# Attention and expert kernel: one row maximum moved a slot up, q's high parts spread over slots, fourth maximum earlier, preamble reordered

## The reference, cut to what matters

```python
x = x + xattn(ctx, layernorm(x), ...)      # x: 2 x 1024 x 256, ctx: 2 x 77 x 256
x = x + ffn(layernorm(x), ...)

# xattn, 16 heads of 64
q = lat @ Wq                               # lat: normalized x
k, v = split(concat([ctx_n, lat], axis=1) @ Wkv)     # 1024 + 77 keys
attn = softmax(q @ k.T / 8)
out = (attn @ v) @ Wout
# ffn: a shared SwiGLU expert, and 32 experts with top-4 routing within 4 of 8 groups, capacity 160
```

## Time and profile before

| | |
|---|---|
| Runs | 1634.35 us median (1633.24 to 1637.85) |
| Profiled execution | 1635.06 us; span 1633.3 us; granted TensorE clock 0.981 on average |
| PE busy | 1511.4 us (93%) |
| PE weight loads | 1060.9 us (65%) |
| DVE busy | 1051.9 us (64%) |
| ACT busy | 798.7 us (49%) |
| POOL busy | 940.4 us (58%) |
| First score product (L939) | at 51.9 us |
| Attention, first to last block | 51.9 to about 1105 us |
| Length of a block | plain 28.4 to 31.4 us, project 36.2 to 37.8 us |
| Work that ended last | PE 66%, DVE 19%, ACT 8% of the span |

### The profile page before, as it was taken

How to read it: one execution, slowest core, us unless ns; L and a number is a source line. 1 busy time by engine, 2 the same in 40 slices (tenths; PEclk the granted TensorE clock), 3 DMA queues, 4 the chain that set the end, 5 groups by cost and what they waited for, 6 DMA issues and landing times.

```text
span 1633.3 us, 23810 instructions
## 1 busy us (share of the span) xinstructions
PE 1511.4 (93%) x8086; PEld 1060.9 (65%) x8086; DVE 1051.9 (64%) x1574; ACT 798.7 (49%) x1501; POOL 940.4 (58%) x751
## 2 busy tenths in 40 slices
PE   3899999999999999999999999988889999999995
PEld 2565555555655555555555555546779999999995
DVE  6556666576666665767767776556756666666662
ACT  3345444544454445544454444534336666666662
POOL 4457666676566665665668768784433433344333
PEclk8899999999999999999999999999999999999998
DMA  3033440000000000000011000111246666667664
GB/s 95 22 81 72 101 91 11 24 15 10 24 15 10 15 10 24 15 11 15 10 28 32 27 28 27 36 39 59 85 159 175 188 185 169 174 186 188 169 174 89
DMA packets 99282, 117.93 MB, mean 72 GB/s; under 512 B 10595, under 2 KB 78181, under 8 KB 99173
## 3 DMA queue, kind: packets, MB, share of 16 engines
q1 hardware_dynamic: 82149, 96.97, 20.4%
q0 software_dynamic: 17056, 19.97, 6.3%
HBM read 74.93 MB, written 35.06 MB: 67 GB/s over the span
## 4 chain that ended last, share of the span: by engine, by line
PE 66%; DVE 19%; ACT 8%; POOL 3%; issue 3%; DMA 1%; SPq 0%; DVEq 0%; ACTq 0%; POOLq 0%
PE ps_o L954 11%; PE ps_t L811 8%; PE ps_m L811 8%; PE ps_st L811 7%; DVE arena_r L1314 7%; PE ps_m L916 7%; PE ps_st L939 5%; PE ps_st L943 4%; ACT arena_r L1574 3%; PE ps_m L848 3%; PE ps_o L848 3%; DVE arena L1325 2%; PE ps_t L974 2%; PE ps_t L1021 2%; PE ps_t L961 2%
## 5 line engine op out<-in xcount | busy, mean ns | idle before, releaser
L751 POOL TENSOR_TENSOR arena<-arena 128x512 f32<-128x512 f32 (+1 forms) x512 | 660.2, 1291 | 337.7 <-ACT arena L1597 300.2
L1597 ACT ACTIVATE arena<-ps_st 128x512 f32<-128x512 f32 (+1 forms) x576 | 329.9, 596 | 460.8 <-PE ps_st L943 426.4
L1314 DVE TENSOR_REDUCE arena_r<-ps_m 128x1 fp32r<-128x1107 f32 x256 | 334.2, 1306 | 182.8 <-PE ps_m L916 180.7
L786 POOL DMA_INDIRECT acc_rows<-arena,ids x96 | 150.8, 1571 | 268.1 <-ACT arena L1660 240.4
L954 PE MATMUL ps_o<-arena 128*64 128x512 f32 (+1 forms) x1152 | 276.5, 606 | 0.0
L939 PE MATMUL ps_st<-arena_r 128*128 128x512 f32 (+1 forms) x576 | 247.2, 429 | 13.9 <-ACT arena L1597 13.9
L943 PE MATMUL ps_st<-arena_r 68*128 68x512 f32 (+2 forms) x576 | 231.1, 401 | 2.5 <-DVE arena_r L1321 1.4
L916 PE MATMUL ps_m<-arena_r 128*128 128x370 f32 x768 | 192.6, 359 | 34.6 <-DVE arena_r L1314 27.1
L916 PEld LDWEIGHTS ps_m<-arena_r 128*128 128x128 f32 x768 | 130.9, 192 | 109.5 <-DVE arena_r L1314 68.5
L939 PEld LDWEIGHTS ps_st<-arena_r 128*128 128x128 f32 (+1 forms) x576 | 106.8, 185 | 108.1 <-ACT arena L1597 83.5
L811 PE MATMUL ps_m<-arena_r 128*128 128x320 f32 (+1 forms) x864 | 164.7, 326 | 2.1 <-DVE arena_r L1404 1.2
(11 more groups left out here) (211 smaller groups left out, 1922.7 us busy)
## 6 DMA issues: line engine op xcount, KB each, us to landing
arena<-in_L_ffn_wg_dram SPq DMA_DIRECT2D x32, 512.0 KB, 4.6
arena<-in_L_ffn_wu_dram SPq DMA_DIRECT2D x32, 512.0 KB, 6.3
arena<-in_L_ffn_wd_dram SPq DMA_DIRECT2D x32, 512.0 KB, 3.8
x_slots<-route SPq DMA_DIRECT2D x5, 2176.0 KB, 12.9
arena<-x_slots SPq DMA_DIRECT2D x32, 272.0 KB, 2.7
arena_r<-arena_r SPq DMA_DIRECT2D x30, 275.2 KB, 3.8
arena<-in_L_xattn_Wkv_dram SPq DMA_DIRECT2D x32, 128.0 KB, 2.4
arena<-x_slots SPq DMA_DIRECT2D x32, 68.0 KB, 2.4
```

Source lines behind the costliest of these rows:

```text
L751: pool.tensor_tensor(total, probsT[0:rows, h, 0, :] if kt == 1 else total, probsT[0:rows, h, kt, :], ALU.add).then_inc(added, 1)
L786: pool.indirect_dma_start(out=dst[:, :], in_=y_sb[par][:, c, 0:w], in_offset=None, compute_op=ALU.add, out_offset=bass.IndirectOffsetOnAxi ...
L1314: dve.tensor_reduce(neg[h][:, c:c + 1], ps_m[:, :, 0:PIECE_W], AX.XY, ALU.max, negate=True)\
L1597: act.activation(probsT[0:rows, h, kt, :], ps_st[0:rows, n % 2, :], ACT.Exp).then_inc(exp_done, 1)
```

## The change

One event moves in every block, three kinds in blocks 0 and 2, one in blocks 1 and 3, the preamble's list is rewritten, "broot" becomes an event of its own (ACT's roots, before part of "bstat"), and POOL's memsets are cut in two: those of the first pair's buffers, then a wait until both halves of z are scaled, then those of the second pair's.

```diff
+        q_high = [nxt("hi", "q", pp, n % 2, (part,)) for part in range(4)]
...
-                 (1, 1): [],
-                 (1, 2): [old("norm", prev), next_max[0]],
+                 (1, 1): [next_max[0]],
+                 (1, 2): [old("norm", prev)],
...
         if project:
...
-            after[0, 5] = project_q() + [q_again] + last_values[:2] + [q_low, own_max[3]]
+            after[0, 4] = [own_max[3]]
+            after[0, 5] = project_q() + [q_again] + last_values[:2] + [q_low]
...
         else:
-            after[0, 0] = [own_max[0]] + project_q()
-            after[0, 1] = [own_max[1]]
-            after[0, 2] = [q_again]
-            after[0, 3] = [own_max[2], q_low]
-            after[0, 4] = last_values[:2]
-            after[0, 5] = [own_max[3]]
+            after[0, 0] = [own_max[0], nxt("q", pp, n % 2)]
+            after[0, 1] = [own_max[1], q_high[0]]
+            after[0, 2] = [q_high[1]]
+            after[0, 3] = [own_max[2]]
+            after[0, 4] = last_values[:2] + q_high[2:]
+            after[0, 5] = [own_max[3], q_low]
...
-    before = [("w", 0), ("kv", 0), ("zn",), ("k", 0, 0), ("hi", "k", 0, 0, (0, 1)), ("q", 0, 0), ("kv", 1),
-              ("lo", "k", 0, 0), ("hi", "q", 0, 0, (0, 1)), ("hi", "q", 0, 0, (2, 3)), ("zc",), ("k", 0, 2),
-              ("lo", "q", 0, 0), ("hi", "k", 0, 2, (0, 1)), ("k", 0, 1), ("lo", "k", 0, 2), ("bstat", 0),
-              ("hi", "k", 0, 1, (0, 1)), ("bstat", 1), ("lo", "k", 0, 1), ("max", 0, 0, 0), ("v", 0, 0),
-              ("max", 0, 0, 1), ("v", 0, 1), ("max", 0, 0, 2), ("v", 0, 2), ("max", 0, 0, 3), ("row", 0, 0)]
+    before = [("w", 0), ("kv", 0), ("zn",), ("k", 0, 0), ("kv", 1), ("hi", "k", 0, 0, (0, 1)), ("k", 0, 1),
+              ("lo", "k", 0, 0), ("hi", "k", 0, 1, (0, 1)), ("q", 0, 0), ("zc",), ("lo", "k", 0, 1), ("k", 0, 2),
+              ("hi", "q", 0, 0, (0, 1)), ("hi", "q", 0, 0, (2, 3)), ("hi", "k", 0, 2, (0, 1)), ("lo", "q", 0, 0),
+              ("lo", "k", 0, 2), ("max", 0, 0, 0), ("v", 0, 0), ("bstat", 0), ("v", 0, 1), ("broot", 0),
+              ("max", 0, 0, 1), ("bstat", 1), ("v", 0, 2), ("broot", 1), ("max", 0, 0, 2), ("max", 0, 0, 3),
+              ("row", 0, 0)]
...
-            for part, value in [
-                    (part.bitcast(F32), value) for h in range(2)
-                    for part, value in [(neg[h], 0.0), (q2[h][OTHER[h], :], 0.0)]
-                    + [pv for b in range(2) for pv in ((k1[b][h][:, KEYS:KEYS + 1], 0.0), (k2[b][h][OTHER[h], :], 0.0),
-                                                       (k2[b][h][MROW[h], :], 1.0))]]:
-                seq.done(pool.memset(part, value))
-                seq.wait()
+            def pair_rows(b):
+                for h in range(2):
+                    for part, value in ((k1[b][h][:, KEYS:KEYS + 1], 0.0), (k2[b][h][OTHER[h], :], 0.0),
+                                        (k2[b][h][MROW[h], :], 1.0)):
+                        seq.done(pool.memset(part.bitcast(F32), value))
+                        seq.wait()
+
+            for h in range(2):
+                for part in (neg[h], q2[h][OTHER[h], :]):
+                    seq.done(pool.memset(part.bitcast(F32), 0.0))
+                    seq.wait()
+            pair_rows(0)
+            pool.sem_inc(pair_consts, 1)
+            pool.wait_ge(z_ready, 2)
+            pair_rows(1)
             pool.sem_inc(pair_consts, 1)
...
-                if kind == "bstat":
+                if kind == "broot":
                     root(6 + a, QT_N, QT_N)
```

## The result

The changed kernel takes **1613.15 us** (median of 4 runs, 1612.70 to 1614.24) against 1634.8 for the kernel before in the runs beside it: ratio 0.9864, 95% interval 0.9852 to 0.9877, so 1.36% faster. The forecast was 1620.8 in 1612.5 to 1629.5. The side was right and the time inside the range, at its edge: 21.6 us were gained where 13.6 were worked out.

The account below looks back on a forecast made before the run. TensorE was taken as the bound, busy 93%, so only waits stopping it count. Terms 5.6 + 0.5 + 6.6 + 4.3 + 0.5 - 3.9 = 13.6 us gave 1620.8 us, range 1612.5 to 1629.5 at 8 in 10.

Parts of the forecast that it names:

- Preamble, start: Start of normalization: six of sixteen memsets wait, so z's second half is ready at 15.1 instead of 17.85, 2.8 us earlier.
- the rule: Trainium skill: a two-SBUF-input DVE instruction is held up by GpSimd reading SBUF, not only writing; so 2.9 us stay.
- the bound that would have eaten 3.9 us: Preamble: five DVE operations beside the moved memsets lose up to 0.78 us each, 3.9 in all, and the gain goes.
- Rival (a): Preamble: memsets are paid in the new place, first maximum at about 36.5, total 1624.3 us; chance 0.12.
- Preamble, order: Rewritten preamble queues: first maximum at 32.8 instead of 40.15, row job at 46.0, 5.6 us gained.
- 1.5 us either way: Preamble: a stretch of PE at 1.2 GHz may fall on the v jobs or not.
- Project blocks: Blocks projecting k (d 1 and 3): fourth maximum a slot up gains 6.6 us, next block's first maximum 4.3.
- The first maximum's term: Project blocks, slot 1 of h 1: it fills PE's hole, 0.45 us in seven blocks, 0.15 in eight; 4.3 us.
- Rival (b): Project blocks turn one wait into another, 10.9 us shrink to 3, total 1628.7 us; chance 0.13.
- (d): The block edits do nothing on balance, savings reappear at DVE's maxima, preamble brings 4, total 1630.4 us; chance 0.06.
- Plain blocks: Blocks d 0 and 2: earlier first maximum gains 0.5 us; q's late low part loses 3.9 in four late blocks.
- the terms' own bounds: The forecast's own range: 2.5 to 8.5 us from the preamble, 4 to 11 from the blocks, giving 1614.9 to 1627.9.

Follow-up runs that it names:

- The row shown at 268.20: From the run that moved only the next block's first maximum a slot up, against the kernel before; ratio 0.9993 (0.9976 to 1.001).

## Why the prediction was right or wrong

**Preamble, start.** Right in each number. The eight scalings are 406 to 416 ns each:

```profile
L1092 DVE TENSOR_SCALAR arena<-x_sb,mv,rstd x8: 406/407/416, 11.8 to 14.7; 128x256 f32<-128x256 f32 x8
L1092 DVE TENSOR_SCALAR arena<-spare,mv,rstd x2: 772/889/1006, 18.9 to 19.8; 77x256 f32<-77x256 f32 x2
```

z was ready at 15.1 us as worked out. Beside the moved memsets the weight split took 0.69 and kvT's low parts 1.29 for two, undisturbed (0.75 and 1.29 before), while the two context scalings took 1.70 instead of 0.73: the rule held against the bound that would have eaten 3.9 us, and the 0.8 of slowing allowed for the scalings was close to the 1.0 that came. Rival (a) is dead.

**Preamble, order.** First maximum 33.63 (32.8 worked out), row job 46.58 (46.0). The sum was 0.8 us too good for this profile, and well within what the seven profiles with this start show: 31.5 to 34.0 and 43.8 to 47.4. So the term of 5.6 is neither missed nor confirmed to a microsecond. The "1.5 us either way" that the forecast gave the clock is about that spread.

**Project blocks.** 11.8 us where 10.9 were worked out: 10.5 in fifteen blocks, and 1.3 in the very last, which has no next maximum and is not in the sum. The fourth maximum measured 6.7 in its own run, where 6.6 was the term. The first maximum's term holds in seven blocks at 0.46 to 0.51 and is near nothing in the rest; on its own it measured nothing. Rival (b) is dead, and the thin margin at exponential 1 held. So is (d): the waits for DVE's maxima did rise, by 4.2 us, but the blocks brought 16.4.

**Plain blocks: the step that failed.** "q's low part ... 0.6 + 1.2 + 0.6 + 1.4 = 3.9 us lost" and "the late q parts are no gain here". The lateness itself came, smaller: the slot after the sum starts 0.66, 0.28, 0.68 and 0.83 us later in the four late blocks, 2.45 in sum, and only the first of them ends later than before. But I followed the freed exponential only along PE, where it meets the third maximum and is worth nothing, and not along POOL, whose chain of additions is timed by that exponential. Some thirteen microseconds further on in the block the additions meet the split on DVE, which is on the path, and in the late turns they stand ahead of POOL's own product, for which PE waits. In turn 6 the split fell from 2.85 to 1.73 and from 3.14 to 1.62 us, which more than pays for the late row. I had the earlier trace rows, 627 to 3189 ns for one and the same operation, used them only as a bound for the preamble, and had even named the additions that read SBUF. The operation that stands on the path with a fivefold spread was the term to work out. Plain blocks came out 7.5 us better than forecast, 4.9 of it in the four late ones and 2.6 in the rest, and that is nearly all of the 8.0 missed. That 1613.15 still lies in the range is luck as far as this term goes: the terms' own bounds ended at 1614.9, and only the allowance beyond them reached it.

## What to carry to other kernels

When one operation on the path has a spread of durations, ask what runs beside it, and follow every edit along that engine too, idle as it may be: a shift of POOL's additions by about a microsecond was worth some 10 us here. Better than to hit the phase is to take the operation off the path: moved into a gap the split lasts 1.0 to 1.5 us in turns 0 to 5, longer than before the move, and still PE's waits for DVE's maxima fell from 30.3 to 18.5 us. Then look at the engine that waits next, which was POOL in the last turns. And before a term is read off one profile, compare kernels that share the code: the same start took 44.4 to 47.9 us.

## What the runs showed of the hardware that I had not expected

- Within attention, stretches of 3.4 us or more at half the clock lie close behind single pauses of PE of 1.3 to 2.9 us, and the block is then up to 1.7 us longer. The row shown at 268.20 is one of four such places in that kernel. But the kernel before had none between 59 and 1083 us, with five pauses of 1.46 to 1.94, and pauses of 2.36 and 2.41 us passed without one in the kernel with the four. The changed kernel has one, at 260.3; with the low part early it is gone there and turn 2's first block has one.
- The same code can have such a stretch in one execution and not in another. The runs of the preamble alone, the memsets alone and the list alone leave the blocks as they were, and all three have one in turn 6, block 2 (at 930 to 932 us), behind a pause of 1.88 us, where the kernel before has 1.87 and none. Which pauses bring it is open; it was not tried by itself.
- After the last block the spans of the kernels here differ by up to 4.6 us for the same code. So sums from two profiles and differences of medians can differ by that much; how much of it is the clock's was not worked out.
- The DVE split with two inputs in SBUF can wait for two additions on POOL in the late turns, where POOL also has the scatters' transfers to issue and its additions follow one another without a gap: in turn 6 of the kernel before it takes 2.85 us from 861.64, beside additions from 861.43 and from 862.66 to 863.93.
